# Nine expert tiles before the last group, the other rows packed into dense tiles, 32 result scatters

## The chip, the cores and the metric

One Trainium2 chip, one of its cores. The metric is device time of one execution in microseconds (us), the median over several runs of the same program. Lower is better.

## The reference

Sixteen sequences of 128 tokens (2048 tokens of width 128) pass through a small language-model tower:

```
h = LN(GLU(conv3(LN(emb[x] + pos))) + LN(emb[x] + pos))
h = h + spiking_attention(LN(h))          # q, k, v thresholded to 0/1, causal, per sequence
h = h + MoE(LN(h))                        # MoE adds its own input too
MoE(xf): probs = softmax(xf @ Wr + br); the 2 largest of 16 experts, weights normalised to sum 1
         expert e: gelu(xf @ W1[e] + b1[e]) @ W2[e] + b2[e], 128 -> 256 -> 128
         y = xf + sum over the 2 chosen of weight * expert(xf)
```

Each token is routed to two experts, so there are 4096 (token, choice) rows of expert work.

## The kernel before

**The front.** The 2048 tokens go through everything up to the routing in four groups of four sequences (512 tokens). Each engine has its program written stage by stage, and the order in which it interleaves the stages of different groups is written out by hand: `front` (L214) sorts all (start time, group, stage) entries of two tables, `EARLY` (L207) and `STAGES` (L208), and each engine runs its own stages in that order. The stages of one group that matter here are `stats3`, `rsqrt3`, `ln3` (the last layer norm), `logits`, `choose` (top-2 of 16), `rank` (each row's rank within its expert, by matmuls with 0/1 matrices), `slot` (`slots_of`, L693: DVE makes the row's slot number) and `scatter` (`scatter_rows`, L426: GpSimd, shown as POOL, issues 8 indirect DMAs of 128 rows each into the DRAM buffer `slots`). A row of `slots` is 132 floats (528 bytes): the normalised token and, in column 128, its place in the result. Each expert has a region of 2176 rows.

**Tables.** After the last group's slots, DVE copies the 16 expert counts to integers (L709), and makes from them the table of full tiles (L711 to L730): for each of up to 32 full tiles of 128 rows its expert and first row. SP and ACT meanwhile write 128 rows of zeros behind each expert's last row (`zero_fill`, L303, 8 experts each), with an out-of-range place, so that the last, partly filled tile of each expert reads defined data.

**The expert loop.** There are `TILES` = 32 + 16 = 48 tiles of 128 rows: 32 that may be full, whose expert is read at run time from `tile_w` into a register (`value_load`, L291, on PE and on DVE), and 16 tails, one for each expert, whose expert is a constant. SP loads tile j into one of 16 buffers `xt` (L352), after it has waited once for all scatters. `experts` (L278) runs a five-stage software pipeline. In step s, each engine does, in this order where it takes part: load the expert of tile s; transpose x of tile s (PE L974), copy it out (ACT L542); copy out the transposed hidden (ACT L552); add b2 of tile s-4 (DVE L770); add b1 of tile s-1 (DVE L764); gelu of tile s-2 (ACT L547); transpose the hidden of tile s-3 (PE L986); second matmul of tile s-4 (PE L995); first matmul of tile s-1 (PE L979). After each tile's L770, POOL scatters its 128 result rows into the DRAM buffer `parts` at the row's place (L444, 48 indirect DMAs; places out of range are dropped).

**The end.** SP waits for all result scatters (L356), reads `parts` back in 8 transfers (L360), ACT, POOL and DVE weight and add the two choices and the residual (L561, L455, L779, L787), and SP stores 4 blocks (L364). The routing weights `w_top` (L746 to L753) and the residual `h0 = h1 + xf` (L741) are made on DVE before the expert loop. On PE, 24 dummy matmuls (L965) run between the table and the first tile.

An engine's instructions run in order. A `wait_ge` holds up everything behind it on that engine; `link` makes the next instruction wait for the one before it.

Of the kernel before, what the change touches and what calls it, by code (L numbers as in the profile page):

```python
# [15 lines left out]
BF16 = mybir.dt.bfloat16  # L16
# [6 lines left out]
P = 128  # L23
# [11 lines left out]
def tower_kernel(nc, x, emb, pos, g1, b1, conv_w, conv_b, g2, b2, Wq, Wk, Wv, Wr, br, W1, fb1, W2, fb2, out):  # L35
# [12 lines left out]
    REGION = T + P  # L48
    DUMMY = EXPERTS * REGION
    SLOTS = DUMMY + P  # L50


    FULL = TOPK * T // P
    TILES = FULL + EXPERTS
    U = 16
    assert TILES % U == 0
    NOWHERE = 1 << 20
# [4 lines left out]
    with ExitStack() as ctx:  # L62
# [3 lines left out]
        def sem(name):  # L66
# [33 lines left out]
        tile_id = sb("tile_id", [P, FULL])  # L100
# [11 lines left out]
        spike_q = sb("spike_q", [P, GROUPS, N], BF16)  # L112
        spike_k = sb("spike_k", [P, GROUPS, N], BF16)
        spike_v = sb("spike_v", [P, GROUPS, N], BF16)
        routed = sb("routed", [P, GROUPS, N], BF16)
        stage = sb("stage", [P, TOPK, GROUPS, GS, ROW])
        LNS = 4
        WARM = 24
# [30 lines left out]
        done_before = sb("done_before", [P, FULL, EXPERTS])  # L149
        skipped = sb("skipped", [P, FULL, EXPERTS])  # L150
        tile_expert = sb("tile_expert", [P, FULL])
        tile_w = sb("tile_w", [P, FULL], I32)
        tile_skip = sb("tile_skip", [P, FULL])
        tile_row_f = sb("tile_row_f", [P, FULL])
        tile_row = sb("tile_row", [P, FULL], I32)
        tail_row = sb("tail_row", [P, EXPERTS], I32)
# [7 lines left out]
        y_sb = work_a[:].rearrange("p g (s d) -> p (g s) d", d=D)  # L164
# [23 lines left out]
        rows_out, zeros_out, dummy_out = map(sem, ("rows_out", "zeros_out", "dummy_out"))  # L188

        xt_in = [sem(f"xt_in{i}") for i in range(U)]  # L190
        placed = [sem(f"placed{i}") for i in range(U)]
        t_xT_psum, t_xT, t_h_psum, t_h, t_act, t_actT_psum, t_actT, t_y_psum, t_y = map(
            sem, ("t_xT_psum", "t_xT", "t_h_psum", "t_h", "t_act", "t_actT_psum", "t_actT", "t_y_psum", "t_y"))
# [7 lines left out]
        def by_seq(ap, n=P):  # L201
# [5 lines left out]
        EARLY = dict(x0=-2, weights=4, stats0=1, rsqrt0=2, ln0=5, xhatT=6, x1T=5, convg=9, conva=13, tanh=13, a=18)  # L207
# [3 lines left out]
                      logits=39.5, choose=41, rank=46, slot=49, scatter=56)  # L211
        EARLY_PERIOD, PERIOD = 13, 16

        def front(**program):  # L214

            order = [(start + EARLY_PERIOD * g, g, stage) for stage, start in EARLY.items() for g in range(GROUPS)]
# [27 lines left out]
        def rsqrt_pool(pool, link, at):  # L244
# [30 lines left out]
        TILE_STEPS = dict(load_expert=0, turn_x=0, evacuate_x=0, first=1, add_b1=1, gelu=2, turn_act=3,  # L275
                          evacuate_act=3, second=4, add_b2=4)
# [25 lines left out]

        def zero_fill(eng, e):  # L303

            n = eng.value_load(count_i[0:1, e:e + 1], min_val=0, max_val=T)
            eng.dma_start(slots[bass.ds(n + e * REGION, P), :], zero_rows[:]).then_inc(zeros_out, 16)

# [3 lines left out]
        def _(sp):  # L311
# [19 lines left out]
            sp.dma_start(slots[DUMMY:DUMMY + P, :], zero_rows[:]).then_inc(dummy_out, 16)  # L331

            sp.wait_ge(count_ready, 1)
            for e in range(EXPERTS // 2):
                zero_fill(sp, e)
# [3 lines left out]
            sp.wait_ge(dummy_out, 16)  # L339
            for j in range(TILES):  # L340
                u = j % U
                if j < FULL:
                    row = sp.value_load(tile_row[0:1, j:j + 1], min_val=0, max_val=DUMMY)
                else:
                    row = sp.value_load(tail_row[0:1, j - FULL:j - FULL + 1], min_val=0, max_val=DUMMY - P)
# [9 lines left out]
            for u in range(U):  # L355
                sp.wait_ge(placed[u], 16 * (TILES // U))  # L356
# [12 lines left out]
        def _(pool):  # L369
# [19 lines left out]
            pool.memset(zeros_e[:], 0.0)  # L389
            pool.memset(causal[:], 1.0)  # L390
# [8 lines left out]
            pool.iota(region_at[:], pattern=[[REGION, EXPERTS]], base=0, channel_multiplier=0,  # L399
                      allow_small_or_imprecise_dtypes=True)  # L400
            pool.iota(tile_id[:], pattern=[[1, FULL]], base=0, channel_multiplier=0,
                      allow_small_or_imprecise_dtypes=True)

            for k in range(TOPK):
                pool.iota(stage[:, k, :, :, ROW_PLACE:ROW_PLACE + 1].bitcast(I32),
                          pattern=[[N, GROUPS], [P, GS], [0, 1]], base=k * T, channel_multiplier=1)
            pool.memset(zero_rows[:, ROW_PLACE:ROW_PLACE + 1].bitcast(I32), NOWHERE).then_inc(consts_ready, 1)
            pool.wait_ge(consts_ready, 2)

# [16 lines left out]
            def scatter_rows(g):  # L426
                pool.wait_ge(staged, g + 1)
                pool.wait_ge(slots_ready, g + 1)
                for s in range(GS):
# [9 lines left out]
            last_place = pool.to_reg(TOPK * T - 1)  # L439

            for j in range(TILES):
                u = j % U
                pool.wait_ge(t_y, j + 1)
                pool.indirect_dma_start(  # L444
                    out=parts, out_offset=bass.IndirectOffsetOnAxis(
                        ap=xt[:, u, ROW_PLACE:ROW_PLACE + 1].bitcast(U32), axis=0),
                    in_=y_sb[:, u, :], in_offset=None, bounds_check=last_place,
                    oob_is_err=False).then_inc(placed[u], 16)
# [9 lines left out]
        def _(act):  # L458
# [70 lines left out]
            act.wait_ge(count_ready, 1)  # L529
            for e in range(EXPERTS // 2, EXPERTS):  # L530
                zero_fill(act, e)


            act.wait_ge(shifted_ready, 1)
# [31 lines left out]
        def _(dve):  # L566
# [77 lines left out]
            def spikes(g):  # L644
                dve.wait_ge(qkv_psum, 3 * g + 1)
                dve.tensor_scalar(spike_q[:, g, :], bank[4][:], Q_THRESH, None, ALU.is_ge)
                dve.wait_ge(qkv_psum, 3 * g + 2)
                dve.tensor_scalar(spike_k[:, g, :], bank[5][:], K_THRESH, None, ALU.is_ge).then_inc(spikes_ready, 1)
                dve.wait_ge(qkv_psum, 3 * g + 3)
                dve.tensor_scalar(spike_v[:, g, :], bank[6][:], V_THRESH, None, ALU.is_ge).then_inc(spike_v_ready, 1)  # L650

            def route_mask(g):
                dve.wait_ge(score_psum, g + 1)
                dve.scalar_tensor_tensor(out=by_seq(routed[:, g, :]), in0=by_seq(bank[5][:]), scalar=MASK_THRESH,
# [38 lines left out]
            def slots_of(g):  # L693
# [7 lines left out]
                                slot_f[:, g, :]).then_inc(slots_ready, 1)  # L701

            front(stats0=stats_x0, rsqrt0=rsqrt_x0, glu=glu, stats1=stats_z, rsqrt1=rsqrt_z, h0=make_h0,
                  stats2=stats_h0, rsqrt2=rsqrt_h0, spikes=spikes, mask=route_mask, stats3=stats_h1, rsqrt3=rsqrt_h1,
                  choose=choose, slot=slots_of)


            dve.wait_ge(count_psum, 1)
            dve.tensor_copy(count_i[:], bank[7][:, 128:128 + EXPERTS]).then_inc(count_ready, 1)  # L709
            dve.wait_ge(count_ready, 1)  # L710
            link(dve.tensor_scalar(tiles_i[:], count_i[:], P.bit_length() - 1, None, ALU.logical_shift_right))  # L711
            link(dve.tensor_copy(tiles_f[:], tiles_i[:]))
            dve.tensor_scalar(skip_rows[:], tiles_f[:], -float(P), float(REGION), ALU.mult, ALU.add)

            dve.scalar_tensor_tensor(out=tail_row[:], in0=tiles_f[:], scalar=float(P), in1=region_at[:], op0=ALU.mult,
                                     op1=ALU.add)
            link(dve.tensor_tensor_scan(tiles_upto[:], tiles_f[:], zeros_e[:], 0.0, ALU.add, ALU.add))

            every = [P, FULL, EXPERTS]
            link(dve.tensor_tensor(done_before[:], tile_id[:].unsqueeze(2).broadcast_to(every),  # L720
                                   tiles_upto[:].unsqueeze(1).broadcast_to(every), ALU.is_ge))
            dve.tensor_tensor(skipped[:], done_before[:], skip_rows[:].unsqueeze(1).broadcast_to(every), ALU.mult)
            link(dve.tensor_reduce(tile_expert[:], done_before[:], AX_X, ALU.add))
            link(dve.tensor_reduce(tile_skip[:], skipped[:], AX_X, ALU.add))


            dve.tensor_scalar(tile_w[:], tile_expert[:], float(EXPERTS - 1), None, ALU.min)
# [296 lines left out]
```

## Time and profile before

| | us |
|---|---|
| median of 3 runs (230.05 to 231.3) | 230.28 |
| span of the profiled execution, first to last instruction | 229.0 |
| TensorE busy, share of the span | 163.2 (71%) |
| VectorE busy | 122.7 (54%) |
| ScalarE busy | 94.2 (41%) |
| GpSimd busy | 100.8 (44%) |

The profiled execution's own time is known by its span; the medians lie 1.28 us above it. Spans and starts in rows are microseconds from the first instruction. PE is TensorE, DVE VectorE, ACT ScalarE, POOL GpSimd, SP SyncE; a name with q (DVEq, SPq) is that engine's sequencer, which decodes instructions, waits, and does register work that isn't counted as busy.

### The profile page before, as it was taken

How to read it: one execution, taken by the hardware profiler on the slowest of the kernel's cores; microseconds unless marked ns; L12 is line 12 of the kernel's file. 1: busy time of each engine (PE TensorE's matmuls, PEld its weight loads, DVE VectorE, ACT ScalarE, POOL GpSimd, SP SyncE). 2: the span in 40 equal slices, each digit the busy share in tenths (PEclk: the TensorE clock that was granted, in tenths of full speed). 3: DMA queues.
4: the chain of work that ended last, by engine and by line, in shares of the span. 5: the costliest groups of instructions: out<-in, count | busy, mean ns of one | idle time of the engine just before them, and what ended most of it. 6: DMA issues, size and time to landing. Idle time of an engine off the chain costs nothing.

```text
span 229.0 us, 3461 instructions
## 1 busy us (share of the span) xinstructions
PE 163.2 (71%) x833; PEld 111.6 (49%) x833; DVE 122.7 (54%) x511; ACT 94.2 (41%) x256; POOL 100.8 (44%) x158
## 2 busy tenths in 40 slices
PE   4859769886989579608926274899999999991000
PEld 1634434563466266405504131588888888870000
DVE  2531356279587863796562762245555566550174
ACT  2131252525560651145123003467777777760240
POOL 5000520502220672057257472057777777777060
PEclk9999967999799965955785569599999999999555
DMA  1799920000000010001001152234344442100576
GB/s 55 225 340 320 410 88 0 4 0 0 1 3 1 12 59 24 0 12 61 24 24 62 49 177 83 59 89 115 106 119 109 121 112 63 20 17 12 150 217 183
DMA packets 23148, 20.18 MB, mean 88 GB/s; under 512 B 3107, under 2 KB 20813, under 8 KB 22874
## 3 DMA queue, kind: packets, MB, share of 16 engines
q1 hardware_dynamic: 19418, 15.16, 22.5%
q0 software_dynamic: 2560, 4.27, 5.7%
q10 hardware_dynamic: 1152, 0.54, 0.8%
q8 instruction: 7, 0.11, 0.2%
q14 instruction: 11, 0.09, 0.1%
HBM read 13.49 MB, written 7.51 MB: 92 GB/s over the span
## 4 chain that ended last, share of the span: by engine, by line
PE 60%; DVE 14%; ACT 7%; DMA 6%; POOL 6%; issue 5%; SPq 1%; DVEq 0%; POOLq 0%; ACTq 0%
PE bank L979 10%; PE bank L995 9%; PE bank L862 9%; PE bank L986 5%; PE bank L831 4%; DVE stats L597 3%; POOL slots L431 3%; PE bank L934 3%; PE bank L899 3%; PE bank L974 3%; DMA work_b<-parts 2%; PE bank L900 2%; PE bank L902 2%; ACT stage L475 2%; PE bank L842 2%
## 5 line engine op out<-in xcount | busy, mean ns | idle before, releaser
L444 POOL DMA_INDIRECT parts<-work_a,xt x48 | 47.2, 983 | 25.8 <-DVE work_a L770 15.8
L431 POOL DMA_INDIRECT slots<-stage,slot_of x32 | 31.6, 987 | 17.8 <-issue 8.9
L862 PE MATMUL bank<-x1T,convw_sb 128*128 128x512 f32 x48 | 29.2, 756 | 2.5 <-ACT x1T L486 2.5
L979 PE MATMUL bank<-w_sb,xtT 128*128 (+1 forms) x96 | 30.1, 396 | 0.0
L995 PE MATMUL bank<-w_sb,act_hT 128*128 (+1 forms) x192 | 29.8, 278 | 0.0
L764 DVE TENSOR_TENSOR hid<-bank,fb_bc 128x256 f32<-128x256 f32 x48 | 20.4, 425 | 13.3 <-PE bank L979 7.7
L995 PEld LDWEIGHTS bank<-w_sb,act_hT 128*128 128x128 f32 x192 | 25.7, 194 | 0.2 <-ACT act_hT L552 0.2
L770 DVE TENSOR_TENSOR work_a<-bank,fb_bc 128x128 f32<-128x128 f32 x48 | 14.0, 292 | 19.3 <-PE bank L995 19.3
L542 ACT ACTIVATE xtT<-bank 128x128 f32<-128x128 f32 x48 | 13.3, 278 | 20.2 <-PE bank L974 20.2
L420 POOL TENSOR_TENSOR work_c<-work_b,g_bc 128x256 f32<-128x256 f32 x8 | 5.7, 723 | 34.9 <-ACT work_b L475 34.9
L986 PE MATMUL bank<-ident,act_h 128*128 128x128 f32 x96 | 19.4, 284 | 0.3 <-ACT act_h L547 0.3
L547 ACT ACTIVATE act_h<-hid 128x256 f32<-128x256 f32 x48 | 19.6, 408 | 0.0
L552 ACT ACTIVATE act_hT<-bank 128x256 f32<-128x256 f32 x48 | 18.4, 384 | 1.9 <-PE bank L986 1.6
L862 PEld LDWEIGHTS bank<-x1T,convw_sb 128*128 128x128 f32 x48 | 10.7, 238 | 14.4 <-issue 12.2
L831 PE MATMUL bank<-ident,stage 128*128 128x128 f32 x16 | 6.0, 409 | 16.3 <-ACT stage L475 15.9
L974 PE MATMUL bank<-ident,xt 128*128 128x128 f32 x48 | 14.2, 297 | 4.1 <-DMA xt<-slots 4.1
L597 DVE BATCH_NORM_STATS2 stats<-bank 128x6 f32<-128x128 f32 x32 | 7.1, 286 | 17.0 <-PE bank L842 13.9
L979 PEld LDWEIGHTS bank<-w_sb,xtT 128*128 128x128 f32 x96 | 15.3, 201 | 0.0
L248 POOL TENSOR_SCALAR rs_work<-mean_var 128x4 f32<-128x4 f32 x3 | 0.7, 234 | 32.8 <-DVE mean_var L600 32.8
L475 ACT ACTIVATE work_b<-bank,rs_work 128x128 f32<-128x128 f32 x32 | 12.0, 459 | 6.8 <-DVE rs_work L241 4.2
L986 PEld LDWEIGHTS bank<-ident,act_h 128*128 128x128 f32 x96 | 10.2, 143 | 5.2 <-ACT act_h L547 1.4
L831 PEld LDWEIGHTS bank<-ident,stage 128*128 128x128 f32 x16 | 2.6, 161 | 20.0 <-ACT stage L475 20.0
(160 smaller groups left out, 272.6 us busy)
## 6 DMA issues: line engine op xcount, KB each, us to landing
xt<-slots SPq DMA_DIRECT2D x48, 66.0 KB, 1.8
w_sb<-in_L_ffn_W_dram SPq DMA_DIRECT2D x1, 2048.0 KB, 9.5
fb_bc<-in_L_ffn_b_dram SPq DMA_DIRECT2D x1, 2048.0 KB, 18.6
fb_bc<-in_L_ffn_b_dram SPq DMA_DIRECT2D x1, 1024.0 KB, 11.2
work_b<-parts SPq DMA_DIRECT2D x4, 256.0 KB, 3.9
work_a<-parts SPq DMA_DIRECT2D x4, 256.0 KB, 5.6
out_dram<-work_c SPq DMA_DIRECT2D x4, 256.0 KB, 2.4
parts<-work_a,xt POOLq DMA_INDIRECT x48, 2.3
```

The costliest lines, as they stand in the source:

```text
L431: pool.indirect_dma_start(out=slots, out_offset=bass.IndirectOffsetOnAxis(ap=slot_of[:, g, k, s:s + 1].bitcast(U32), axis=0), in_=stage[:, ...
L444: pool.indirect_dma_start(out=parts, out_offset=bass.IndirectOffsetOnAxis(ap=xt[:, u, ROW_PLACE:ROW_PLACE + 1].bitcast(U32), axis=0), in_= ...
L475: act.activation(dst[s], src[s], ACT.Identity, scale=rs_work[:, 8, at, s:s + 1], bias=rs_work[:, 9, at, s:s + 1]).then_inc(normed[which], 1)
L547: act.activation(act_h[:, b, :], hid[:, b, :], ACT.Gelu).then_inc(t_act, 1)
L552: act.activation(act_hT[:, b, :], bank[4 + b][:, 0:HID], ACT.Copy).then_inc(t_actT, 1)
L764: dve.tensor_tensor(hid[:, b, :], bank[2 + b][:, 0:HID], flat(fb1_bc[:, expert_of(j), :]), ALU.add).then_inc(t_h, 1)
L831: last = pe.transpose(blocks(dst, s), src[s], ident[:])
L862: last = pe.matmul(by_seq(acc[:]), convw_sb[:, w, half * D:(half + 1) * D], x1T[:, g, :, w:w + L], start=(w == 0), stop=(w == TAPS - 1))
L974: pe.transpose(bank[b][:, 0:P], xt[:, u, 0:D], ident[:]).then_inc(t_xT_psum, 1)
L979: pe.matmul(bank[2 + b][:, 0:HID], xtT[:, b, :], flat(w1_sb[:, expert_of(j), :]), start=True, stop=True).then_inc(t_h_psum, 1)
L986: last = pe.transpose(bank[4 + b][:, c * P:(c + 1) * P], act_h[:, b, c * P:(c + 1) * P], ident[:])
L995: last = pe.matmul(bank[6 + b][:, 0:D], act_hT[:, b, c * P:(c + 1) * P], flat(w2_sb[:, expert_of(j), c, :]), start=(c == 0), stop=(c == 1))
```

## The change

With 16 experts, 3 of 4 groups scattered early and 128 rows a tile, the new constants are `EARLY` = 9 (the number of full tiles that three groups are sure to give), `LATE` = 32 - 9 = 23 dense tiles, `LAG` = 15, `UNITS` = 38 and `TILES` = 9 + 38 = 47. What was called `EARLY` is now `FIRST`.

- The table of full tiles is made on DVE in a new stage `tally` (start 50), of the counts of the first three groups, in the third group's turn. It lists nine tiles. SP loads them once the first three groups' scatters have landed.
- All 16 zero fills are issued by SP, after `count_ready` of the third group. Each writes 5 x 128 rows from the third group's last row on. The last group's scatters wait for all of them.
- All rows that the nine tiles don't take are thought of as one dense list of 23 tiles, sorted by expert. A dense tile that holds rows of several experts is worked on once for each of them: a unit is a pair of tile and expert, 38 at most. A unit reads 128 rows in its expert's region that line up with the dense tile; rows that aren't its expert's are masked to zero (the mask scales the gelu's input and b2), and its result is added into the dense tile.
- After the last group's slots, DVE works out each unit's facts (expert, dense tile, first row, first and last valid row), PE spreads them over partitions, and DVE makes `unit_i` and `mask` in step 2 of the expert loop.
- In the loop DVE has, for each unit, a second `value_load` and two more instructions (`gather`). There are 32 result scatters, with no bounds check. The weights `w_top` are computed behind the loop. The 24 dummy matmuls are gone. Four buffers shrink from 4 to 2 groups (`g % 2`).

```diff
     FULL = TOPK * T // P
-    TILES = FULL + EXPERTS
+    SOON = GROUPS - 1
+    EARLY = -(-(TOPK * SOON * N - EXPERTS * (P - 1)) // P)
+    LATE = FULL - EARLY
+    LAG = EXPERTS - 1
+    UNITS = LATE + LAG
+    TILES = EARLY + UNITS
+    CLEAR = (TOPK * (T - SOON * N) // TOPK + P) // P
...
-        TILE_STEPS = dict(load_expert=0, turn_x=0, evacuate_x=0, first=1, add_b1=1, gelu=2, turn_act=3,
-                          evacuate_act=3, second=4, add_b2=4)
+        TILE_STEPS = dict(load_expert=0, turn_x=0, evacuate_x=0, list_units=1, first=1, add_b1=1, gelu=2, turn_act=3,
+                          evacuate_act=3, second=4, add_b2=4, gather=4)
...
             def load_expert(j):
-                if j < FULL:
-                    e = eng.value_load(tile_w[0:1, j:j + 1], min_val=0, max_val=EXPERTS - 1)
-                    of[j] = bass.ds(e, 1)
+                if j < EARLY:
+                    at = tile_w[0:1, j:j + 1]
                 else:
-                    of[j] = slice(j - FULL, j - FULL + 1)
+                    if j == EARLY:
+                        eng.wait_ge(units_ready, 1)
+                    at = unit_i[0:1, E_ID, j - EARLY:j - EARLY + 1]
+                of[j] = bass.ds(eng.value_load(at, min_val=0, max_val=EXPERTS - 1), 1)
...
# SP
+            sp.wait_ge(pads_out, 16)
             sp.wait_ge(count_ready, 1)
-            for e in range(EXPERTS // 2):
-                zero_fill(sp, e)
+            for e in range(EXPERTS):
+                n = sp.value_load(count_i[0:1, e:e + 1], min_val=0, max_val=SOON * N)
+                sp.dma_start(slots[bass.ds(n + (P + e * REGION), CLEAR * P), :].rearrange("(c p) w -> p c w", p=P),
+                             zero_rows[:].unsqueeze(1).broadcast_to([P, CLEAR, ROW])).then_inc(zeros_out, 16)
...
                 if j == 0:
-                    sp.wait_ge(rows_out, 16 * TOPK * SEQS)
+                    sp.wait_ge(rows_soon, 16 * TOPK * GS * SOON)
-                if j == FULL:
+                if j == EARLY:
                     sp.wait_ge(zeros_out, 16 * EXPERTS)
+                    sp.wait_ge(rows_last, 16 * TOPK * (SEQS - GS * SOON))
                 if j >= U:
-                    sp.wait_ge(placed[u], 16 * (j // U))
+                    sp.wait_ge(t_place, j - U + 1)
...
# POOL
             def scatter_rows(g):
                 pool.wait_ge(staged, g + 1)
                 pool.wait_ge(slots_ready, g + 1)
+                if g == SOON:
+                    pool.wait_ge(zeros_out, 16 * EXPERTS)
...
-            for j in range(TILES):
+            for d in range(FULL):
+                at = d if d < EARLY else d + 1
+                if d < EARLY:
+                    pool.wait_ge(t_part, d + 1)
+                    pool.wait_ge(t_place, d + 1)
+                else:
+                    pool.wait_ge(t_y, d - EARLY + 1 + LAG)
...
# ACT, in gelu(j), units only
+                act.activation(act_h[:, b, :], hid[:, b, :], ACT.Gelu,
+                               scale=mask[:, j - EARLY:j - EARLY + 1]).then_inc(t_act, 1)
...
# DVE: tally holds L709 to L730 over 9 tiles; facts of the units behind the front; then in the loop
+            def add_b2(j):
+                b = j % 2
+                dve.wait_ge(t_y_psum, j + 1)
...
+                tile = dve.value_load(unit_i[0:1, E_SHIFT, j - EARLY:j - EARLY + 1], min_val=0, max_val=LATE)
+                dense_of[j] = tile
+                dve.scalar_tensor_tensor(out=y_part[:, b, :], in0=flat(fb2_bc[:, expert_of(j), :]),
+                                         scalar=mask[:, j - EARLY:j - EARLY + 1], in1=bank[6 + b][:, 0:D],
+                                         op0=ALU.mult, op1=ALU.add).then_inc(t_part, 1)
+
+            def gather(j):
+                u, b = j % U, j % 2
+                if j < EARLY:
+                    dve.tensor_copy(place[:, j:j + 1], xt[:, u, ROW_PLACE:ROW_PLACE + 1]).then_inc(t_place, 1)
+                    return
+                at = dense_of[j]
+                dve.wait_ge(t_place, j)
+                listed = place[:, bass.ds(at + EARLY, 1)]
+                dve.scalar_tensor_tensor(out=listed, in0=xt[:, u, ROW_PLACE:ROW_PLACE + 1],
+                                         scalar=mask[:, j - EARLY:j - EARLY + 1], in1=listed,
+                                         op0=ALU.mult, op1=ALU.add).then_inc(t_place, 1)
+                dve.wait_ge(t_part, j + 1)
+                if j > EARLY:
+                    dve.wait_ge(t_y, j - EARLY)
+                tile = flat(dense[:, bass.ds(at, 1), :])
+                dve.tensor_tensor(tile, tile, y_part[:, b, :], ALU.add).then_inc(t_y, 1)
+
+            experts(load_expert=load_expert, add_b2=add_b2, add_b1=add_b1, list_units=list_units, gather=gather)
```

## Rows read from the trace of the kernel before

**Rows 1.** Chain of waits: share of the span by engine.
```profile
PE 60%; DVE 14%; ACT 7%; DMA 6%; POOL 6%; issue 5%; SPq 1%; DVEq 0%; POOLq 0%; ACTq 0%
```

**Rows 2.** The same chain in time order: start, duration (us), what.
```profile
138.14 3.08 DMA slots<-stage,slot_of
...
211.16 2.11 DMA parts<-work_a,xt
```

**Rows 3.** Busy time in stretches: engines, granted PE clock, DMA share, GB/s.
```profile
8.00:29.00 21.00, 15.54 (x59) 8.91 (x58) 7.89 (x39) 5.39 (x13) 3.24 (x14) 1.00 1.03 340
45.00:58.00 13.00, 10.56 (x57) 6.91 (x56) 10.95 (x52) 5.11 (x13) 1.42 (x2) 0.98 0.00 0
96.00:116.00 20.00, 11.51 (x47) 7.17 (x47) 14.18 (x72) 6.99 (x16) 9.12 (x10) 0.66 0.08 27
...
133.00:134.00 1.00, 1.00 (x3) 0.33 (x3) 1.00 (x4) 0.00 (x0) 1.00 (x1) 0.50 0.64 186
143.32:150.00 6.68, 6.17 (x21) 4.36 (x22) 1.32 (x4) 3.11 (x10) 0.00 (x0) 0.53 0.26 61
150.00:202.00 52.00, 52.00 (x385) 44.81 (x384) 30.59 (x86) 38.71 (x128) 39.34 (x40) 1.00 0.35 93
```

**Rows 4.** Timeline: start, us; third group's slots, table of tiles, POOL's first last-group scatter.
```profile
115.51 0.17 DVE L700 CAST slot_of<-slot_f 128x8 int32<-128x8 f32 x1
...
128.51 0.17 DVE L709 CAST count_i<-bank 128x16 int32<-128x16 f32 x1 [0.29 <-PE bank L955]
...
129.01 0.96 POOL L431 DMA_INDIRECT slots<-stage,slot_of  x1 [2.76 <-DVE slot_of L700]
...
129.53 0.69 DVE L720 TENSOR_TENSOR done_before<-tile_id,tiles_upto 128x512 f32<-128x512 f32 x1
...
132.66 0.18 DVE L730 TENSOR_SCALAR tile_row<-tile_row_f 128x32 int32<-128x32 f32 x1
```

**Rows 5.** Groups of instructions: count, busy us, mean ns, idle before.
```profile
L764 DVE TENSOR_TENSOR hid<-bank,fb_bc 128x256 f32<-128x256 f32 x48 | 20.4, 425 | 13.3 <-PE bank L979 7.7
L770 DVE TENSOR_TENSOR work_a<-bank,fb_bc 128x128 f32<-128x128 f32 x48 | 14.0, 292 | 19.3 <-PE bank L995 19.3
L241 DVE SCALAR_TENSOR_TENSOR rs_work<-mean_var,rs_work 128x4 f32<-128x4 f32 x13 | 2.2, 168 | 0.4
```

**Rows 6.** DMA queue of ACT (8 zero fills): packets, MB, share of 16 engines.
```profile
q10 hardware_dynamic: 1152, 0.54, 0.8%
```

**Rows 7.** Timeline of SP: its eight zero fills.
```profile
129.69 8.13 SPq L306 DMA_DIRECT2D slots<-zero_rows  x8
```

**Rows 8.** Value load on DVE's sequencer, whole run: ns min/median/max.
```profile
L291 DVEq TENSOR_LOAD <-tile_w x32: 299/303/556, 140.1 to 182.3; - x32
```

**Rows 9.** One value load, at 165 us: duration ns and start.
```profile
L291 DVEq TENSOR_LOAD <-tile_w x1: 299/299/299, 165.1 to 165.1; - x1
L291 DVEq FUSED_REGOPS  x1: 190/190/190, 165.4 to 165.4; - x1
L291 DVEq SEQ_ASSERT  x1: 23/23/23, 165.6 to 165.6; - x1
```

**Rows 10.** The next instruction behind it, L770, with its register operation.
```profile
L770 DVEq FUSED_REGOPS  x1: 57/57/57, 165.7 to 165.7; - x1
L770 DVE TENSOR_TENSOR work_a<-bank,fb_bc x1: 292/292/292, 165.8 to 165.8; 128x128 f32<-128x128 f32 x1
```

**Rows 11.** Timeline: first tile's transpose, steady loop, last tile.
```profile
143.32 0.48 PE L974 MATMUL bank<-ident,xt 128*128 128x128 f32 x1 [3.57 <-DMA xt<-slots]
...
160.95 0.29 DVE L770 TENSOR_TENSOR work_a<-bank,fb_bc 128x128 f32<-128x128 f32 x1 [0.36 <-PE bank L995]
...
162.16 0.29 DVE L770 TENSOR_TENSOR work_a<-bank,fb_bc 128x128 f32<-128x128 f32 x1 [0.36 <-PE bank L995]
...
206.84 0.29 DVE L770 TENSOR_TENSOR work_a<-bank,fb_bc 128x128 f32<-128x128 f32 x1 [0.45 <-PE bank L995]
```

**Rows 12.** Waits at the end of the kernel: us in total, times, longest.
```profile
DVE work_d L779 <- DMA work_b<-parts: 11.4, 4, 9.2
```

More of the change, by code:

```diff
@@ L148, in tower_kernel @@
         skip_rows = sb("skip_rows", [P, EXPERTS])
[L149 to L156, printed above, removed]
+        done_before = sb("done_before", [P, EARLY, EXPERTS])
+        skipped = sb("skipped", [P, EARLY, EXPERTS])
+        tile_expert = sb("tile_expert", [P, EARLY])
+        tile_w = sb("tile_w", [P, EARLY], I32)
+        tile_skip = sb("tile_skip", [P, EARLY])
+        tile_row_f = sb("tile_row_f", [P, EARLY])
+        tile_row = sb("tile_row", [P, EARLY], I32)
+        tiles_prior = sb("tiles_prior", [P, EXPERTS])
+        tiles_open = sb("tiles_open", [P, EXPERTS])
+        taken = sb("taken", [P, EXPERTS])
+        region_left = sb("region_left", [P, EXPERTS])
+        PICK = 6
+        E_ID, E_SHIFT, E_ROW, E_FROM, E_TO, E_ONE = range(PICK)
+        left = sb("left", [P, EXPERTS])
+        left_upto = sb("left_upto", [P, EXPERTS])
+        left_from = sb("left_from", [P, EXPERTS])
+        ends_i = sb("ends_i", [P, 2, EXPERTS], I32)
+        ends_at = sb("ends_at", [P, 2, EXPERTS], I32)
+        spans = sb("spans", [P, EXPERTS])
+        units_of = sb("units_of", [P, EXPERTS])
+        units_upto = sb("units_upto", [P, EXPERTS])
+        units_prior = sb("units_prior", [P, EXPERTS])
+        past = sb("past", [P, EXPERTS])
+        mine = sb("mine", [P, EXPERTS])
+        facts = sb("facts", [P, PICK, EXPERTS])
+        picked = sb("picked", [P, PICK, EXPERTS])
+        per_unit = sb("per_unit", [P, PICK])
+        of_unit = sb("of_unit", [P, PICK])
+        moved = sb("moved", [P, PICK])
+        valid = sb("valid", [P, PICK])
+        spread = sb("spread", [UNITS, PICK - 1, UNITS])
+        unit_i = sb("unit_i", [P, 3, UNITS], I32)
+        from_row = sb("from_row", [P, UNITS])
+        mask = sb("mask", [P, UNITS])
+        ones_f = sb("ones_f", [UNITS, P])
         xt = sb("xt", [P, U, ROW])
@@ L210, in tower_kernel @@
                       h1out=31.7, stats3=34, rsqrt3=34.1, ln3=37, copy=43, xfT=38.5, xfTout=39,
-                      logits=39.5, choose=41, rank=46, slot=49, scatter=56)
-        EARLY_PERIOD, PERIOD = 13, 16
+                      logits=39.5, choose=41, base=44, rank=46, slot=49, tally=50, scatter=56)
+        FIRST_PERIOD, PERIOD = 13, 16
         def front(**program):
-            order = [(start + EARLY_PERIOD * g, g, stage) for stage, start in EARLY.items() for g in range(GROUPS)]
+            order = [(start + FIRST_PERIOD * g, g, stage) for stage, start in FIRST.items() for g in range(GROUPS)]
             order += [(start + PERIOD * g, g, stage) for stage, start in STAGES.items() for g in range(GROUPS)]
@@ L436, in _ @@
             front(rsqrt0=rsqrt_x0, scale=scale_g2, scatter=scatter_rows)
-            last_place = pool.to_reg(TOPK * T - 1)
-            for j in range(TILES):
-                u = j % U
-                pool.wait_ge(t_y, j + 1)
+            for d in range(FULL):
[5 more added lines that the diff above has]
+                    pool.wait_ge(t_y, d - EARLY + 1 + LAG)
                 pool.indirect_dma_start(
[L445 to L448, printed above, removed]
+                    out=parts, out_offset=bass.IndirectOffsetOnAxis(ap=place[:, at:at + 1].bitcast(U32), axis=0),
+                    in_=soon_y[:, d, :] if d < EARLY else dense[:, at - EARLY, :], in_offset=None).then_inc(scattered, 16)
             pool.wait_ge(base_ready, 1)
@@ L527, in _ @@
                   xfTout=evacuate_xfT)
[L529 to L534, printed above, removed]
+            act.wait_ge(shifted_ready, GROUPS)
             act.activation(exps[:], shifted[:], ACT.Exp)
@@ L722, in _ @@
[L722 to L727, printed above, removed]
-            link(dve.scalar_tensor_tensor(out=tile_row_f[:], in0=tile_id[:], scalar=float(P), in1=tile_skip[:],
-                                          op0=ALU.mult, op1=ALU.add))
@@ L742, in _ @@
-            link(last)
+                  choose=choose, base=early_base, slot=slots_of, tally=tally)
+            dve.wait_ge(count_psum, 2)
+            link(dve.scalar_tensor_tensor(out=left[:], in0=taken[:], scalar=-float(P),
+                                          in1=bank[3][:, 0:EXPERTS], op0=ALU.mult, op1=ALU.add))
+            link(dve.tensor_tensor_scan(left_upto[:], left[:], zeros_e[:], 0.0, ALU.add, ALU.add))
+            dve.tensor_tensor(ends_i[:, 0, :], left_upto[:], left[:], ALU.subtract)
@@ new lines, in _ @@
+            dve.tensor_tensor(left_from[:], left_upto[:], left[:], ALU.subtract)
+            link(dve.tensor_scalar(ends_i[:, 1, :], left_upto[:], float(P - 1), None, ALU.add))
+            link(dve.tensor_scalar(ends_at[:], ends_i[:], P.bit_length() - 1, None, ALU.logical_shift_right))
+            link(dve.tensor_tensor(spans[:], ends_at[:, 1, :], ends_at[:, 0, :], ALU.subtract))
+            link(dve.scalar_tensor_tensor(out=units_of[:], in0=left[:], scalar=0.0, in1=spans[:], op0=ALU.is_gt,
+                                          op1=ALU.mult))
@@ new lines, in _ @@
+            link(dve.tensor_tensor_scan(units_upto[:], units_of[:], zeros_e[:], 0.0, ALU.add, ALU.add))
+            link(dve.tensor_tensor(units_prior[:], units_upto[:], units_of[:], ALU.subtract))
+            dve.tensor_scalar(past[:], units_upto[:], part_id[:], None, ALU.is_le)
+            link(dve.tensor_tensor(facts[:, E_SHIFT, :], ends_at[:, 0, :], units_prior[:], ALU.subtract))
+            link(dve.scalar_tensor_tensor(out=facts[:, E_FROM, :], in0=facts[:, E_SHIFT, :], scalar=-float(P),
+                                          in1=left_from[:], op0=ALU.mult, op1=ALU.add))
@@ new lines, in _ @@
+            dve.scalar_tensor_tensor(out=mine[:], in0=units_prior[:], scalar=part_id[:], in1=past[:], op0=ALU.is_le,
+                                     op1=ALU.subtract)
+            dve.tensor_tensor(facts[:, E_TO, :], facts[:, E_FROM, :], left[:], ALU.add)
+            link(dve.tensor_tensor(facts[:, E_ROW, :], region_left[:], facts[:, E_FROM, :], ALU.subtract))
+            link(dve.tensor_tensor(picked[:], mine[:].unsqueeze(1).broadcast_to([P, PICK, EXPERTS]), facts[:], ALU.mult))
+            link(dve.tensor_reduce(per_unit[:], picked[:], AX_X, ALU.add))
@@ L907, in score @@
                 for s in range(GS):
-                    last = pe.matmul(blocks(bank[5], s), blocks(spike_k[:, g, :], s), blocks(spike_q[:, g, :], s),
+                    last = pe.matmul(blocks(bank[5], s), blocks(spike_k[:, g % 2, :], s), blocks(spike_q[:, g % 2, :], s),
                                      start=True, stop=True)
@@ L961, in _ @@
             pe.wait_ge(table_ready, 1)
-            for _ in range(WARM):
-                pe.matmul(bank[5][:], ident_b[:], ones_b[:].unsqueeze(1).broadcast_to([P, 4, P]), start=True, stop=True)
             pe.wait_ge(w1_in, 16)
@@ L980, in first, with list_units @@
                           start=True, stop=True).then_inc(t_h_psum, 1)
+            def list_units(j):
+                if j == 1:
+                    pe.wait_ge(unit_facts, 1)
+                    pe.matmul(bank[6][:, 0:(PICK - 1) * UNITS], ones_f[:],
+                              spread[:].rearrange("u q n -> u (q n)"), start=True, stop=True).then_inc(unit_psum, 1)
             def turn_act(j):
```

214 lines of the change are left out of this document (136 added, 78 removed).

## The prediction

> **What bounds the kernel now.** I read the chain of waits first: PE holds 60% of it [rows 1]. Then the stretches: from 150 to 202 us PE is busy for all of 52.00 us at a granted clock of 1.00, its 2.4 GHz level [rows 3]. A tile has 9 matmuls (1 + 2 + 2 + 4) and 385 ran there, so a tile takes 52.00 x 9 / 385 = 1.22 us; DVE's adds come 1.21 apart [rows 11]. Ahead of the loop lies a stretch in which PE has no tile: the last group's first scatter starts at 129.01 [rows 4], its last at 138.14 and lands 3.08 later, at 141.22, and the first tile is transposed at 143.32 [rows 2, 11]. Behind the loop the last add ends at 206.84 + 0.29 = 207.13 [rows 11], the last result scatter starts at 211.16 and lands at 213.27 [rows 2], and 229.0 - 213.27 = 15.73 us of reading back and combining follow. The span of 229.0 is 1.28 us under the median of the runs, 230.28; I add 1.28 at the end.
>
> So the change aims at two things: the idle stretch, and POOL's backlog of 213.27 - 207.13 = 6.1 us.
>
> **Part 1: tally on DVE.** The table goes between the third group's slots (L700, ends 115.68) and the last group's `stats3`, on the path to the last slots. Before, it took from 128.51 to 132.84, 4.33 us [rows 4]. It has four operations over 32 x 16 elements (0.69 one of them); over 9 x 16 = 144 they are near the 0.29 of a 128-column operation [rows 5], so 1.6 less. Three small operations, the row offset and the per-group subtractions add about 0.8. Of 3.5 some 0.47 falls into DVE's wait for h1. I take **+3.05**, bounds 2.4 and 3.9. The last slots are ready 3.05 later, and POOL's first scatter could start at 132.1. The moved `h0` adds and the new constants (9 operations on POOL of at most 0.2, a 3072-column clear) lie in idle time at the front; if that cover is gone, 0.7 each.
>
> **Part 2: zero fills.** All on SP, from count_ready at about 116.2; the first issue came 1.0 behind it before (count copied at 128.69, fill issued at 129.69), so 117.2. They write 16 x 640 = 10240 rows, 5.4 MB, where 2048 rows went before. ACT's queue moved 1152 packets in 0.8% of 16 x 229.0 us, 25 ns each [rows 6]; 10240 such packets take 16.3 us on 16 engines. From the stretches: 186 GB/s at a share of 0.64 is 290 GB/s at full share, 340 GB/s were reached at 8 to 29 us [rows 3]: 16 to 18.6 us. The third group's eight scatters (0.5 MB) share the engines, 1.8 us. So the fills have landed at 117.2 + 18.1 + 2.1 (a landing, as of the last result scatter) = **137.4**; by the bounds 134.5 to 139. The other bound is issue: 16 fills of 128 rows were issued by two queues in 8.13 us [rows 7], 0.51 for 128 rows; were that a price for rows, 80 x 0.51 = 41 us. I take the bandwidth, since one issue there moved no more than its 128 rows and the engines were at 0.64.
>
> The last scatters wait for the fills: first at 137.4 + 0.8 = 138.2, that is 9.2 later than before; everything up to the first tile that needs them moves along, so **the first unit is transposed at 143.32 + 9.2 = 152.5**. Queued behind POOL's wait is nothing else. On SP the nine tile loads stand behind the fills: the first lands at about 139.3. Nine steps from a cold start take at most 9 x 1.22 + the slow start, until about 151: hidden in the scatters. The early tiles therefore cost nothing, and take nothing off: they run only in time that the fills and the 3.05 added.
>
> **Part 3: the units on DVE, the main term.** A `value_load` is work of the sequencer, which nothing behind it on DVE can pass. The load of a tile's expert starts at 165.1 with 0.299, then a register operation of 0.190 and a check of 0.023, and the next instruction's register operation is at 165.7 [rows 9, 10]: 0.62 us. Before, it lay in DVE's slack: one of them, 0.42 and 0.29 of adds in 1.22. A unit has two, one at the step's head and one behind the wait for the second matmul: 1.24 us, alone more than PE's 1.22. To it comes, for each of the four instructions with a register address, 0.12 (register operation 0.057 at 165.7, instruction at 165.8 and the next free after it [rows 10]), 0.48; two more register operations for the in-place operands, 0.2; five waits at about 0.03, 0.15. **2.07 us a unit.** DVE's datapath (0.42 + 0.35 + 0.17 + 0.29 = 1.23 [rows 5]) runs beside it. Floor: no extra register operations or waits, 1.72. Ceiling: if the datapath holds the sequencer, 1.24 + 0.12 + 0.7 of adds ahead of the last one, 2.1; with PE at its low clock 2 x 1.22 = 2.44 (below).
>
> PE has slack then, and the loop over ACT and PE back to DVE spans two steps, so neither adds. ACT's gelu with a scale from memory is worth at most 0.1 in 0.3 of idle time.
>
> Steps: 9 to 12 have one load, 4 x 1.22 = 4.9: to 157.4, and step 13's second matmul makes it 157.9 for DVE. Steps 13 to 46, with two loads: 34 x 2.07 = 70.4. Steps 47 to 50, with one: 4 x 1.45 = 5.8. The last add ends at 157.9 + 70.4 + 5.8 = **234.1**. Before: 207.13.
>
> The Trainium skill, "DMA: Bandwidth & Descriptors", section "Latency and other measured facts", gives such a register load from memory a floor of about 600 ns. The trace differs: 299 to 303 ns, and only the first one, a first use, is 556. By the page's figure a unit would take 2.07 + 2 x 0.3 = 2.67.
>
> **Part 4: behind the loop.** POOL keeps up (one scatter in about 1.28, dense tile k is released by unit k + 15), so only the last one is left: 0.3 to its start, 2.11 to its landing, in place of 6.14. The weights (1.9) and an h0 add (0.7) now stand behind the loop on DVE, inside its wait of 9.2 for `parts` [rows 12], which shrinks to 5.4: hidden. End: 234.1 + 0.3 + 2.1 + 15.73 = 252.2, plus 1.28 = **253.5 us**. The dummy matmuls' going costs a slow start of the early tiles, hidden as above.
>
> **Rivals.**
> A. *DVE keeps PE's pace.* If the second value load costs nothing (it overlaps the adds in the queue), units take 1.22: last add at 152.5 + 37 x 1.22 + 6.5 (143.32 to 207.13 less 47 x 1.22) = 204.1, 0.7 for the gather, 1.3 of POOL backlog, 2.4 + 15.73: 224.3, measured 225.6, faster by 2%. For it: before, the load never showed. Against: there was only one, with its 0.62 in 0.36 of waiting plus 0.42 of an add. The kernel gets slower once a unit costs more than about 1.35 on DVE: (230.28 - 225.6) / 34 = 0.14 over 1.22.
> B. *PE falls to 1.2 GHz.* At 2.07 a unit PE is busy for 59%. A stretch with 58% had a granted clock of 0.66, but its gaps were long; one with 81% kept 0.98 [rows 3]. At the low level a tile costs 2.44 and PE is full: + 34 x 0.37 = 12.6, 266 us. Against: it would be full, and the clock rose at 150 us after such a stretch (0.53 from 143.32 [rows 3]). A mixture is likelier than all of it.
> C. *Each value load costs its first price*, 0.556 [rows 8]: + 0.51 a unit, 271 us. The skill's 600 ns would give about 274.
> D. *Fills at issue price*: landed at 117.2 + 41 = 158, + 20: 274 us. Against: part 2.
> That the early tiles don't overlap is not a rival with a price of its own: they would add 9 x 1.22 = 11 us, 264, and nothing queued speaks for it.
>
> **How the numbers follow.** The forecast (DVE's sequencer at 1.75 to 2.3 a unit) 0.75, A 0.10, B 0.07, C 0.04, D 0.04. Units at 1.72 and fills at 134.5 give 239; part of B gives 265. The range of 239 to 266 leaves out A, C and D. 0.5% (1.2 us) is about what a measurement tells from no change: faster 0.09, same 0.01, slower 0.90.
>
> **What would show it.** Right: DVE's adds of the units 2.0 to 2.2 us apart, two register loads on DVE's sequencer in each step; PE waits for DVE, its busy share in the loop near 60%; the last-group scatters start at 137 to 139 behind the fills; nine tiles done by 151. Wrong: units 1.2 us apart with PE full (A), a granted clock near 0.5 in the loop (B), fills beyond 145 (D), or stats3 of the last group not about 3 us later.

## The result, and the profile after

The changed kernel takes 258.93 us (median of 4 runs, 258.06 to 262.41) against 230.17 for the kernel before, measured beside it: 1.124 times the time, 95% interval 1.117 to 1.131. Forecast were 253.5 us and 239 to 266. The profiled execution has a span of 256.9 us, where the sum gave 252.2. On another chip the changed kernel came out at 258.39. Some executions of every kernel run about one or two per cent longer at a lower granted clock; the medians here count them, the ratios and intervals leave them out.

The chain of waits of the changed kernel, by engine, stands against [rows 1]:

```profile
PE 28%; DVE 19%; DVEq 13%; issue 11%; SPq 9%; DMA 8%; ACT 5%; POOL 4%; POOLq 0%; ACTq 0%
```

PE went from 60% to 28%, and DVE's sequencer, which had 0%, holds 13%; "issue", time in which an engine waited for nothing that the profile shows, rose from 5% to 11%. The waits say the same from the other side (engine, line, what it waited for: us in total, times, longest):

```profile
DVE y_part L877 <- issue: 27.6, 33, 1.0
...
POOL slots L491 <- DMA slots<-zero_rows: 21.4, 1, 21.4
...
ACT act_h L607 <- DVE hid L862: 17.3, 34, 0.8
...
PE bank L1130 <- ACT act_h L607: 16.4, 35, 0.8
```

DVE's datapath stood idle 33 times for nothing that another engine owed it, ACT waits for DVE, and PE for ACT. And POOL waited once, for 21.4 us, for the zero fills.

**The units.** The timeline of DVE, in the middle of the loop (start, us; against [rows 11]):

```profile
192.23 0.35 DVE L877 SCALAR_TENSOR_TENSOR y_part<-fb_bc,mask,bank 128x128 f32<-128x128 f32 x1 [1.24 <-PE bank L1141]
192.50 0.42 DVE L862 TENSOR_TENSOR hid<-bank,fb_bc 128x256 f32<-128x256 f32 x1
192.83 0.21 DVE L890 SCALAR_TENSOR_TENSOR place<-xt,mask,place 128x1 f32 x1
192.96 0.28 DVE L897 TENSOR_TENSOR dense<-dense,y_part 128x128 f32 x1
194.12 0.35 DVE L877 SCALAR_TENSOR_TENSOR y_part<-fb_bc,mask,bank 128x128 f32<-128x128 f32 x1 [0.88 <-issue]
```

From 192.23 to 194.12 is 1.89 us, where [rows 11] has 1.21. The four operations fill the first 1.01 us; then DVE is idle for 0.88. What the sequencer does in one unit (another one, duration ns and start; L335 loads the expert of a later unit, L875 the dense tile of the one whose b2 is added at L877):

```profile
L335 DVEq TENSOR_LOAD <-unit_i x1: 303/303/303, 212.1 to 212.1; - x1
L335 DVEq FUSED_REGOPS  x1: 190/190/190, 212.5 to 212.5; - x1
L335 DVEq SEQ_ASSERT  x1: 23/23/23, 212.7 to 212.7; - x1
```

```profile
L875 DVEq TENSOR_LOAD <-unit_i x1: 299/299/299, 212.8 to 212.8; - x1
L875 DVEq FUSED_REGOPS  x1: 190/190/190, 213.1 to 213.1; - x1
L875 DVEq SEQ_ASSERT  x1: 23/23/23, 213.3 to 213.3; - x1
```

```profile
L877 DVEq FUSED_REGOPS  x1: 64/64/64, 213.4 to 213.4; - x1
L877 DVE SCALAR_TENSOR_TENSOR y_part<-fb_bc,mask,bank x1: 348/348/348, 213.5 to 213.5; 128x128 f32<-128x128 f32 x1
...
L897 DVEq FUSED_REGOPS  x1: 57/57/57, 213.9 to 213.9; - x1
```

The two loads stand end to end, from 212.1 to 213.4, with no wait between. The register operations of the four instructions follow, at 213.4, 213.5, 213.7 and 213.9, and the next load starts at 214.0: the sequencer is taken up for the whole 1.9 us. The first unit's add (L877) starts at 168.84 and the last one's at 238.26; of the 37 distances most are 1.87 to 1.91, four are 2.23 to 2.25, and the last four, with one load, 1.25 to 1.65.

**PE in the loop.** Stretch of 60 us (columns as in [rows 3]; its row there is 150 to 202):

```profile
170.00:230.00 60.00, 45.45 (x279) 33.02 (x279) 31.57 (x124) 32.58 (x94) 15.32 (x16) 1.00 0.21 53
```

The clock stayed at 1.00, and 279 matmuls in 60.00 us, 9 a unit, are 1.94 us a unit. PE's share is 76%, where the forecast had "near 60%": each matmul is booked at 0.163 us here and at 0.135 in [rows 3]. The ends of matmuls are modelled, so the count is the safer number.

**The fills.** The stretch, and the issues with their median time to landing; then SP's and POOL's timeline (against [rows 3, 4, 7]):

```profile
118.00:146.00 28.00, 5.14 (x22) 3.77 (x22) 9.99 (x66) 4.78 (x10) 6.12 (x7) 0.53 1.19 218
```

```profile
slots<-zero_rows SPq DMA_DIRECT2D x16, 330.0 KB, 7.0
```

```profile
116.74 23.20 SPq L375 DMA_DIRECT2D slots<-zero_rows  x16
...
130.57 0.17 DVE L761 CAST slot_of<-slot_f 128x8 int32<-128x8 f32 x1
...
147.38 0.96 POOL L491 DMA_INDIRECT slots<-stage,slot_of  x1 [21.43 <-DMA slots<-zero_rows]
```

The last group's slots are ready at 130.7; POOL starts at 147.38, 18.4 us later than the 129.01 of [rows 4]. The fills took from 116.74 to 146.6, 29.9 us, with the DMA engines full (1.19) at only 218 GB/s. SP issued the last one at 139.23, and it landed 7.35 later: the engines were behind, not SP.

**The tally and the end**, timeline of the changed kernel (against [rows 2, 4, 12]):

```profile
115.49 0.17 DVE L783 CAST count_i<-bank 128x16 int32<-128x16 f32 x1
...
118.67 0.87 DVE L658 BATCH_NORM_STATS2 stats<-h 128x6 f32<-128x128 f32 x4
...
238.75 0.29 DVE L897 TENSOR_TENSOR dense<-dense,y_part 128x128 f32 x1
...
239.33 1.15 POOL L506 DMA_INDIRECT parts<-dense,place  x1 [0.30 <-DVE dense L897]
...
245.00 0.35 DVE L918 SCALAR_TENSOR_TENSOR work_d<-work_b,w_top,h 128x128 f32<-128x128 f32 x1 [3.59 <-DMA work_b<-parts]
```

### The profile page after: what moved, and what is told of

Its sections match the earlier page's. It is cut to its first block, busy times and chain, and to the rows that moved or that the text cites. A ratio compares the mean times of both kernels' runs of the same rounds, so it can differ in the third digit from the quotient of the medians.

```text
span 256.9 us, 3937 instructions
## 1 busy us (share of the span) xinstructions
PE 164.5 (64%) x803; PEld 108.1 (42%) x803; DVE 137.4 (53%) x627; ACT 98.5 (38%) x253; POOL 87.7 (34%) x151
## 4 chain that ended last, share of the span: by engine, by line
PE 28%; DVE 19%; DVEq 13%; issue 11%; SPq 9%; DMA 8%; ACT 5%; POOL 4%; POOLq 0%; ACTq 0%
PE bank L1001 8%; DVEq L875 7%; DVE y_part L877 5%; DVEq L335 4%; SPq L374 4%; SPq L375 3%; DVE dense L897 3%; PE bank L970 3%; DMA slots<-zero_rows 3%; PE bank L1038 2%; DVE stats L658 2%; POOL slots L491 2%; PE bank L1039 2%; DMA work_a<-parts 2%; PE bank L1073 2%
## 5 line engine op out<-in xcount | busy, mean ns | idle before, releaser
L491 POOL DMA_INDIRECT slots<-stage,slot_of x32 | 31.3, 978 | 37.3 <-DMA slots<-zero_rows 21.4
L506 POOL DMA_INDIRECT parts<-dense,place x23 | 22.2, 966 | 48.8 <-DVE dense L897 48.8
L877 DVE SCALAR_TENSOR_TENSOR y_part<-fb_bc,mask,bank 128x128 f32<-128x128 f32 x38 | 13.2, 347 | 33.3 <-issue 27.6
L1130 PE MATMUL bank<-ident,act_h 128*128 128x128 f32 x94 | 20.5, 300 | 16.4 <-ACT act_h L607 16.4
L1116 PE MATMUL bank<-w_sb,xtT 128*128 x94 | 29.8, 400 | 0.0
L1141 PE MATMUL bank<-w_sb,act_hT 128*128 x188 | 29.7, 281 | 0.1
L862 DVE TENSOR_TENSOR hid<-bank,fb_bc 128x256 f32<-128x256 f32 x47 | 19.7, 419 | 18.0 <-PE bank L1116 16.7
L607 ACT ACTIVATE act_h<-hid,mask 128x256 f32<-128x256 f32 x38 | 19.3, 507 | 17.3 <-DVE hid L862 17.3
L1141 PEld LDWEIGHTS bank<-w_sb,act_hT 128*128 128x128 f32 x188 | 24.9, 193 | 0.9 <-issue 0.3
L597 ACT ACTIVATE xtT<-bank 128x128 f32<-128x128 f32 x47 | 12.4, 264 | 23.5 <-PE bank L1111 23.5
L1111 PEld LDWEIGHTS bank<-ident,xt 128*128 128x128 f32 x47 | 6.8, 146 | 28.4 <-DMA xt<-slots 20.5
```

The costliest lines, as they stand in the source:

```text
L491: pool.indirect_dma_start(out=slots, out_offset=bass.IndirectOffsetOnAxis(ap=slot_of[:, g, k, s:s + 1].bitcast(U32), axis=0), in_=stage[:, ...
L506: pool.indirect_dma_start(out=parts, out_offset=bass.IndirectOffsetOnAxis(ap=place[:, at:at + 1].bitcast(U32), axis=0), in_=soon_y[:, d, : ...
L607: act.activation(act_h[:, b, :], hid[:, b, :], ACT.Gelu, scale=mask[:, j - EARLY:j - EARLY + 1]).then_inc(t_act, 1)
L862: dve.tensor_tensor(hid[:, b, :], bank[2 + b][:, 0:HID], flat(fb1_bc[:, expert_of(j), :]), ALU.add).then_inc(t_h, 1)
L877: dve.scalar_tensor_tensor(out=y_part[:, b, :], in0=flat(fb2_bc[:, expert_of(j), :]), scalar=mask[:, j - EARLY:j - EARLY + 1], in1=bank[6 ...
L1111: pe.transpose(bank[b][:, 0:P], xt[:, u, 0:D], ident[:]).then_inc(t_xT_psum, 1)
```

## The experiments

**A third load.**

```diff
                 dense_of[j] = tile
+                dve.value_load(unit_i[0:1, E_ROW, j - EARLY:j - EARLY + 1], min_val=0, max_val=SLOTS - P)
```

> The changed kernel with a third value load for each unit on DVE, right behind the second; its value is not used. Theory S (DVE's sequencer sets the pace of the units, 1.89 us each): a load is 0.62 us of the sequencer, so the units come 2.5 us apart and the time rises by 34 x 0.62 = 21 us, from 258.9 to 280. Rival L (the pace is the latency of the loop DVE add, gelu, transpose, second matmul, with room on the sequencer): the load falls partly into waiting, the pace rises to less than 2.2 and the time to less than 270.

Measured: 279.2 and 284.1 us in two executions. The units come 2.50 to 2.52 apart, 1.89 + 0.62:

```profile
199.71 0.42 DVE L862 TENSOR_TENSOR hid<-bank,fb_bc 128x256 f32<-128x256 f32 x1
...
202.22 0.42 DVE L862 TENSOR_TENSOR hid<-bank,fb_bc 128x256 f32<-128x256 f32 x1
```

In this unit the three loads start at 200.0, 200.6 and 201.2 and the add's register operation at 201.8, with no wait between. A load of which nothing is used costs its full 0.62 us in every unit. There is no slack on that sequencer: theory S holds, rival L falls.

**The fills in long runs** (the edit shortened).

```diff
-  slots[...CLEAR * P rows].rearrange("(c p) w -> p c w", p=P), zero_rows[:] broadcast to [P, CLEAR, ROW]
+  slots[...CLEAR * P rows].rearrange("(p c) w -> p (c w)", p=P), dense[:] (zeros till the loop), 5 x 132 floats
```

> The changed kernel with the same 16 zero fills of 640 rows, but each partition writes its 5 rows as one run of 2640 bytes, in place of 5 runs of 528 bytes. Theory R (the fills take 29.9 us, twice the forecast, because of the price of a 528-byte run, and the last group's scatters wait for them): 5.4 MB at 340 GB/s take 16 us, the scatters start at 134 instead of 147.4, and the time falls by 13, to 246. Rival B (writing to DRAM is bound by bytes at 200 GB/s): no change, 259. Rival I (bound by SP's issues, 1.45 us each): no change, 259.

Measured: 248.72 us (ratio to before 1.081, interval 1.076 to 1.086), 10.2 less. SP's first fill goes out at 117.44 and POOL starts at 138.97; 0.8 before that, at 138.2, the fills have landed: 20.7 us in place of 29.9, at 300 GB/s. SP's issues, the stretch, and POOL's start:

```profile
117.44 18.50 SPq L376 DMA_DIRECT2D slots<-dense  x16
slots<-dense SPq DMA_DIRECT2D x16, 330.0 KB, 2.8
```

```profile
118.00:138.00 20.00, 5.14 (x22) 3.78 (x22) 10.62 (x68) 4.78 (x10) 6.71 (x7) 0.53 0.84 300
```

```profile
138.97 0.96 POOL L492 DMA_INDIRECT slots<-stage,slot_of  x1 [12.32 <-DMA slots<-dense]
```

The same bytes in a fifth of the runs: so neither bytes nor the 16 issues bound the fills of the changed kernel, which rules out rivals B and I there. R holds in direction, with 10.2 of its 13. The rest is SP: the engines are now at 0.84, each fill lands 2.8 us behind its issue, where it was 7.0, and SP takes 18.5 us to issue the 16, each behind its own value load. With long runs the issues are the bound, as rival I had it, and 300 GB/s is their pace and not the engines' limit. One thing isn't separated: the edit also changes the source (five rows of `dense` in place of one row read five times) and which addresses a partition writes.

**The table behind the last group's rsqrt.** `tally=50` becomes `tally=50.2`.

> The changed kernel with the table of tiles made behind the last group's rsqrt instead of ahead of its stats. If the fills gate the last scatters, as the trace says (POOL waited 21.4 us for them), the count comes 3.5 us later, the fills end 3.5 later, and the time rises to 262.5 although the last group's slots are ready 2.5 us earlier. If the last group's chain on DVE were the gate (the forecast's part 1 as a cost of its own), the time would fall by 2.5, to 256.5.

Measured: 258.69 (1.131, interval 1.122 to 1.139), no change; both numbers missed. The count comes 2.5 us later, the slots 3.7 earlier (126.9), and POOL starts at 147.43, as before:

```profile
119.23 21.48 SPq L375 DMA_DIRECT2D slots<-zero_rows  x16
...
147.43 0.96 POOL L491 DMA_INDIRECT slots<-stage,slot_of  x1 [22.40 <-DMA slots<-zero_rows]
```

The fills gate, so the tally's 2.5 us on the last group's chain cost nothing in the changed kernel. The fills ended at the same time though they began 2.5 later, in 27.4 us for 29.9. Less sharing of the engines with the third group's scatters could be the reason, but it isn't shown: in the profiles of the third load and of the one load (below), where all eight of those scatters ran beside the fills as in the changed kernel, the fills took 28.1 and 27.4 us. The time of the same fills differs between executions by as much as the edit moved them, so this run can't price the count's delay.

**One load for each unit.** Units are numbered so that tile = unit - expert; the expert's register then gives the address. The last unit number would be 39, which is beyond the end of the list and is never run. The edit, shortened:

```diff
-  ends_i[1] = left_upto + P - 1;  units_of = (left > 0) * spans
+  ends_i[1] = left_upto;          units_of = spans + 1
-  tile = dve.value_load(unit_i[0:1, E_SHIFT, ...], min_val=0, max_val=LATE)
+  tile = (register of the expert) + (LATE - unit)      # dense tiles in reverse order, as the scatters take them
```

> The changed kernel without the second value load: the units are numbered so that dense tile = unit - expert always (an expert has a unit for each tile that its stretch touches, ends included, 38 units still), and DVE gets the dense tile from the expert's register by an addition in the address. The result is the reference's. Theory S: the sequencer needs 1.89 - 0.62 = 1.27 us a unit, PE 1.22, so the units come 1.27 to 1.3 apart, and the time falls by 34 x 0.6 = 20, to 238.5. Rival L (loop latency): the units stay above 1.6 apart and the time above 249. If the masked gelu, the two more DVE adds or the gather cost time of their own, it shows here as a pace above 1.3.

Measured: 236.69 (1.029, interval 1.025 to 1.033), 22.2 less for the removal of one value load. Most units come 1.28 to 1.32 apart, and PE is nearly always busy again:

```profile
170.00:210.00 40.00, 39.75 (x271) 31.52 (x271) 30.33 (x121) 31.67 (x90) 14.70 (x16) 1.00 0.29 78
```

So the masked gelu, the two more adds and the gather together cost 0.06 to 0.1 us a unit over PE's 1.22. Which of them costs it isn't taken apart: PE's matmuls hold 45% of the chain of waits from 180 to 200 us, where before they held all of it (155 to 195), and DVE, its sequencer and gaps hold most of the rest. A sequencer that needs 1.89 - 0.62 = 1.27 us a unit is still a little slower than PE.

**The clear made early.**

```diff
-            (pads; wait for count_ready; 16 fills of 5 x 128 rows)
+            whole = slots.rearrange("(p a b) w -> a p (b w)", p=P, b=21)
+            for a in range(13):
+                sp.dma_start(whole[a], dense[...] (21 x 132 zeros)).then_inc(zeros_out, 16)
...
-                if g == SOON:
+                if g == 0:
                     pool.wait_ge(zeros_out, ...)
```

> The changed kernel with no fills behind the count: all of the slots buffer is zeroed early, in 13 transfers whose runs are 11088 bytes, issued at about 20 us behind the weights, and only the first group's scatters wait for it. If the fills' wait is what holds the last scatters, they start at 131.4 (slots ready at 130.6) instead of 147.4, the nine tiles run from 131 to about 146 beside them, and the time falls by 14, from 258.9 to 245. Rival: 18.4 MB at 290 GB/s end at 95 us instead of 80, POOL holds the first group's scatters and behind them the fourth group's scaling, the front gets up to 5 us later and half of the gain is lost: 250.

Measured: 244.27 (1.067, interval 1.059 to 1.075), 14.7 less, or 13 by the ratios. The clear of 18.4 MB runs at 422 GB/s beside the front and is over before the first group's scatters (78.03; 77.17 before), and the last group's start as soon as their slots are there:

```profile
50.00:70.00 20.00, 16.89 (x72) 9.62 (x72) 15.39 (x83) 10.95 (x24) 4.29 (x16) 0.91 1.01 422
```

```profile
131.91 0.95 POOL L486 DMA_INDIRECT slots<-stage,slot_of  x1 [5.60 <-DVE slot_of L756]
```

**All three, and the early tiles held back.** The second of these adds, before tile 0's load, a wait for the last group's scatters.

> One value load for each unit, the early clear, and the table made behind the last group's rsqrt. The result is the reference's. If the two costs are independent, the time is 258.9 - 22 (one load, measured) - 14 (clear) - 2.5 (table off the path, which nothing gates any more) = 220.5, 4% under the kernel before. Rival: POOL becomes the end's bound. It has 8 + 9 + 23 scatters of 1.26 us from 129 on, but waits for unit 15; if it is busy when the last unit is done, the end comes up to 4 us later: 225.

> The same as the one with both, but the nine early tiles' loads also wait for the last group's scatters, so that they don't run beside them. This prices the change's idea. If the overlap is worth what the idea says, nine tiles at 1.22 to 1.3 us less what the pipeline's slow start hides: 9 to 12 us more than the kernel with both, about 231. If something else (POOL, the clock at the start) takes the gain back, less than 6 us more.

Measured: 221.53 us with all three (ratio 0.965, interval 0.959 to 0.970; five of six executions between 220.06 and 222.35, the sixth 782.79) and 231.99 (1.008, interval 1.004 to 1.012) with the early tiles held back. In the first, the last group's scatters start at 128.58, the first tile is transposed at 129.08 and the first unit at 143.60; PE has 320 matmuls in 48 us:

```profile
129.08 0.47 PE L1110 MATMUL bank<-ident,xt 128*128 128x128 f32 x1 [2.12 <-DMA xt<-slots]
...
143.60 0.31 PE L1110 MATMUL bank<-ident,xt 128*128 128x128 f32 x1
```

```profile
150.00:198.00 48.00, 47.29 (x320) 37.25 (x320) 36.70 (x144) 37.05 (x105) 20.11 (x21) 1.00 0.27 73
```

```profile
201.02 0.96 POOL L507 DMA_INDIRECT parts<-dense,place  x1 [0.30 <-issue]
```

The costs add up nearly as if independent: 258.93 - 22.2 - 14.7 leaves 222.0, and 221.53 is 0.5 less; the 2.5 expected of the table don't show in full. The rival of POOL as the end's bound shows in small: the last add ends at 199.28 and POOL, still busy with the scatter before, starts the last one at 201.02, 1.7 behind it, where the changed kernel has 0.3. Holding the tiles back costs 10.5 us: the idea of the change is worth that, once nothing else eats it. And with them held back the kernel takes 0.8% longer than the one before: the dense tiles and the 32 scatters, without the overlap, gave no gain.

**Once more, on another chip.**

> The changed kernel itself, unedited, on the chip on which the next one runs. All theories: 258.9 again, 1.124 times the kernel before; it gives the experiments a comparison on one chip.

> The kernel with one load, the early clear and the later table once more, because one of its six executions took 783 us. If that was a disturbance from outside, all executions lie between 219 and 224 and the ratio to the kernel before is 0.9645 again; if the kernel brings it about, a long execution shows again.

Measured: 258.39 for the changed kernel (executions from 255.44 to 260.38, ratio 1.115, interval 1.107 to 1.123, which overlaps the first one's), and 221.17 (0.965, interval 0.960 to 0.971) for the one with all three, its six executions between 220.66 and 223.78. The single execution of 783 us did not come again; what it was stays open.

## Why the prediction was right, and by how much its terms were off

The forecast, slower because DVE's sequencer is given two value loads in each unit, was right in its mechanism, and the third load and the one load show it from both sides: 2.51, 1.89 and 1.30 us a unit with three, two and one. Rival A would need the load to hide; rival B a low clock, and the loop's clock was 1.00; rival C's high price was seen only in single cases: of the 76 loads of units on DVE's sequencer the longest took 0.415, and the median was 0.30. Rival D's sign, fills beyond 145, did come, but not by its cause: SP issued the last fill at 139.2, the DMA engines were full, and with a fifth of the runs the same 16 issues took 18.5 us.

- *Part 1.* +3.05 forecast; `stats3` starts at 118.67 where it was 116.15, so +2.5. The third group's slots came 0.3 earlier in this execution (115.20 for 115.51), so the table itself cost 2.8. But it gated nothing, since the fills came later still.
- *Part 2, the worst term.* Fills landed at 137.4 by forecast, 146.6 in fact, so POOL's start moved by 9.2 more. The step that failed divided 186 GB/s by a share of 0.64, and took 25 ns a packet from a queue in light traffic [rows 3, 6]. With the engines full, 10240 runs in about 28 us (29.9 less 1.8 for the scatters) are 28 x 16 / 10240 = 44 ns each. Part 2 also said that the early tiles are done by 151: they started at 146.82 for 139.3, and were hidden all the same: the first unit was transposed at 160.66, and PE had waited 1.32 us for its rows.
- *Part 3.* 2.07 forecast, 1.89 measured, 1.94 with the few longer steps. The two loads were 1.24 as forecast; the extra register operations for in-place operands (0.2) don't exist, as there is one per instruction. From step 13 on the sum had 76.2 us to the last add; it took 70.9 (168.1, the first unit's second load, to 239.04), 5.3 less.
- *Part 4.* From the last add (239.04) to the landing 2.7 for 2.4; the tail 15.2 for 15.73; the weights were hidden, with 3.59 of DVE's wait left.

The span's miss of 4.7 is + 10.2 - 5.3 (units) + 0.3 - 0.5. The 10.2 is how much later than 157.9 the first unit's second load came: 8.2 are in the first unit's transpose (160.66 for 152.5, the fills), and 2.0 in the steps from there to its add, where PE once waited 0.89 for rows. The two large terms cancel by half: that the total came closer than its terms was luck.

## What to carry to other kernels

Count what an engine's sequencer has to do in one step of a loop, not only its busy time: DVE was busy for half of the loop and still set its pace, and one register load a unit less gave back 22 us. Where a register holds one index, look for a numbering in which the other follows from it by an addition. Before a bulk write is put on the critical path, price it by the length of its runs under full load, and ask whether it can be done at a time when the DMA queues are empty, even at three times the bytes.

## What was not expected of the hardware

The same queue wrote the same buffer at very different rates: with the engines full, 218 GB/s in runs of 528 bytes (share 1.19) and 422 in runs of 11088 (share 1.01). Runs of 2640 bytes went at 300 with the share at 0.84, and there SP's issues set the pace. The Trainium skill, "DMA: Bandwidth & Descriptors", section "Specifications", puts the smallest transfer for line rate at 512 bytes; runs of 528 bytes here got about half of the rate of long ones. The runs of 528 bytes don't start at round addresses, and whether that or their length sets the price was not tried.

In all the kernels with units, single steps of DVE are 0.35 us longer (2.25 for 1.89, 1.66 for 1.30). With three loads a unit it is every seventh step, with two every eighth or ninth, with one every tenth or eleventh, about 18, 16 and 14 us apart. So it doesn't come at a fixed distance in time; whether it goes by the number of instructions was not tried, and its cause stays open.
